# Cross-attention and feed-forward on one core: value tiles double-buffered across chunks, x converted in halves

## The reference

```
q  = (M @ Wq.T).reshape(512, 8, 64).transpose(1, 0, 2)
kv = x @ Wkv.T + bkv                       # x: 6250 x 256
k, v = jnp.split(kv, 2, axis=-1)           # each to (8, 6250, 64)
sim  = einsum('hid,hjd->hij', q, k) * 64 ** -0.5
attn = softmax(where(mask, sim, -1e9), axis=-1)
out  = einsum('hij,hjd->hid', attn, v)     # back to (512, 512)
m = layer_norm(out @ Wo.T + bo + M)
z = layer_norm(relu(m @ W1.T + b1) @ W2.T + b2 + m)
```

## Time and profile before

| | us |
|---|---|
| median of 3 runs | 763.78 (762.9 to 764.46) |
| the profiled execution | 757.08 |
| its span in the trace | 754.7 |
| PE, DVE, ACT, POOL busy in the span | 648.0, 552.9, 366.1, 243.4 |
| first reduction of a score (start of chunk 0) | 30.31 |
| start of the last chunk | 521.07 |

### The profile page before, as it was taken

How to read it: one execution, slowest core, us unless ns; L and a number is a source line. 1 busy time by engine, 2 the same in 40 slices (tenths; PEclk the granted TensorE clock), 3 DMA queues, 4 the chain that set the end, 5 groups by cost and what they waited for, 6 DMA issues and landing times.

```text
span 754.7 us, 11237 instructions
## 1 busy us (share of the span) xinstructions
PE 648.0 (86%) x3382; PEld 401.9 (53%) x3382; DVE 552.9 (73%) x688; ACT 366.1 (49%) x658; POOL 243.4 (32%) x293
## 2 busy tenths in 40 slices
PE   4867989898898989898989989898989659799995
PEld 3654545554455555455555445554545315578884
DVE  4496799778986898779987899689977732534333
ACT  4454555546555555455564555555554411333332
POOL 2221542227320532245222632054222430522223
PEclk9978999999999999999999999999999869799998
DMA  7066599857896689849986799668874981022221
GB/s 289 1 174 144 126 222 246 221 138 178 216 263 145 148 214 256 187 106 222 249 225 146 172 219 263 144 150 206 211 171 122 301 217 45 28 92 103 83 83 56
DMA packets 52504, 127.96 MB, mean 170 GB/s; under 512 B 15744, under 2 KB 16256, under 8 KB 52224
## 3 DMA queue, kind: packets, MB, share of 16 engines
q1 hardware_dynamic: 41728, 101.97, 52.6%
q10 hardware_dynamic: 10752, 25.70, 13.5%
HBM read 23.80 MB, written 1.05 MB: 33 GB/s over the span
## 4 chain that ended last, share of the span: by engine, by line
PE 49%; SPq 17%; DVE 13%; issue 8%; DMA 8%; ACT 3%; POOL 0%; DVEq 0%; ACTq 0%; POOLq 0%
SPq L335 16%; PE tail L831 12%; PE slot L804 10%; PE tail L729 9%; DVE st L658 7%; DMA pt<-st 7%; PE slot L882 6%; PE slot L890 6%; PE slot L729 5%; DVE prob L648 3%; ACT val L519 1%; DMA wq_raw<-in_wq 1%; PE slot L763 1%; PE tail L838 1%; DVE stats L682 1%
## 5 line engine op out<-in xcount | busy, mean ns | idle before, releaser
L513 ACT ACTIVATE prob<-prob,negmax 128x896 f32<-128x896 f32 x224 | 233.7, 1043 | 239.5 <-DVE negmax L648 236.4
L648 DVE CUSTOM_DVE_ANT_0 prob<-slot,lower,negmax_old 128x896 f32<-128x896 f32 x224 | 249.0, 1149 | 77.8 <-PE slot L804 68.7
L658 DVE STREAM_TRANSPOSE st<-prob 128x1792 f32<-128x1792 f32 x112 | 228.5, 2041 | 22.1 <-DMA pt<-st 20.4
L831 PE MATMUL tail<-pt,val 128*64 128x512 f32 x784 | 191.0, 622 | 20.5 <-DMA pt<-st 10.3
L804 PE MATMUL slot<-k_hi,q_hi 64*128 64x448 f32 x448 | 98.0, 429 | 34.8 <-DVE negmax L648 34.8
L831 PEld LDWEIGHTS tail<-pt,val 128*64 128x64 f32 x784 | 52.2, 142 | 125.3 <-issue 105.7
L804 PEld LDWEIGHTS slot<-k_hi,q_hi 64*128 64x128 f32 x448 | 44.6, 190 | 101.9 <-issue 93.8
L804 PE MATMUL slot<-k_hi,q_lo 64*128 64x448 f32 x448 | 87.4, 379 | 0.0
L804 PE MATMUL slot<-k_lo,q_hi 64*128 64x448 f32 x448 | 86.8, 377 | 0.0
L413 POOL TENSOR_TENSOR total<-total,alpha 128x8 f32<-128x8 f32 x28 | 5.7, 205 | 225.3 <-ACT alpha L550 225.3
L426 POOL TENSOR_TENSOR k_lo<-k_raw,k_hi 128x896 fp32r<-128x896 f32 x27 | 57.0, 2110 | 3.9 <-POOL k_hi L423 0.2
(11 more groups left out here) (110 smaller groups left out, 832.1 us busy)
## 6 DMA issues: line engine op xcount, KB each, us to landing
pt<-st SPq DMA_DIRECT2D x672, 112.0 KB, 3.0
pt<-st ACTq DMA_DIRECT2D x224, 112.0 KB, 3.4
w_raw<-in_w SPq DMA_DIRECT2D x32, 256.0 KB, 2.8
x_raw<-in_x SPq DMA_DIRECT2D x6, 896.0 KB, 5.8
mask_raw<-in_mask SPq DMA_DIRECT2D x7, 448.0 KB, 5.3
mt_raw<-in_mt SPq DMA_DIRECT2D x2, 512.0 KB, 7.8
wq_raw<-in_wq SPq DMA_DIRECT2D x2, 512.0 KB, 8.5
wo_raw<-in_wo SPq DMA_DIRECT2D x1, 1024.0 KB, 5.5
```

Source lines behind the costliest of these rows:

```text
L513: nc.scalar.activation(unit, unit, ACT.Exp, bias=negmax[:, p, u:u + 1], scale=-1.0, accum_out=psumrow[:, p, u:u + 1]).then_inc(exp_done, 1)
L648: nc.vector.tensor_tensor_reduce(out=prob[:, i % 2, h].rearrange("p (b n) -> p b n", b=2), in0=slot[:, j, :, :HALF], in1=lower[:, i].rearr ...
L658: nc.vector.transpose(st[:, g].rearrange("p b k (t i) -> p k b t i", t=2)[:, :, :, t2], prob[:, i % 2].rearrange("p h (k b i) -> p (h k) b ...
L831: last = nc.tensor.matmul(outT[DH * h:DH * h + DH], val[:, i, head(p, h)], moving, start=(i == 0), stop=(i == KT - 1))
```

## The change

The lists of rounds are new. `val` gets three more tiles (`TWICE` = 3). Value tiles 0, 1 and 2 have a second place that is used in odd chunks (`val_at`), so their copies wait only for the weighted sums of the chunk before the last one. N0 is V0 of the next chunk, done in the last round of this one, and P0 is V0 of the very first chunk. V1 to V6 then stand one to a round. All engine programs are given the chunk's parity, and the loop over chunks is unrolled by two: chunks 0, 1, a loop of two passes with two chunks each, and chunk 6.

`x_raw` has half its size. The next chunk's x comes in two DMAs of 448 KB (R0 in p0r0, R1 in p2r2). GpSimd converts the first half (J0) in p2r1 behind K and ahead of L, the second (J1) in p2r3. R1 waits until the first half has been converted. At the start of the kernel the second half lands in `x_late`, memory that is used for something else afterwards.

F and A of pairs 0 and 2 go from r1 to r2. In pair 2, W0 to W6 are spread over all four rounds. After the last chunk's values the loads of the two bias rows get a wait on `pv_done`, and two small tiles change places in memory.

```diff
+TWICE = 3
 ROUNDS = (
-    ('S E0 E1 W0 W1 W2 X M1 R',
-     'S E0 E1 Z F K H L A X B1',
-     'S E0 E1 W3 W4 W5 W6 C X M0 Q',
-     'S E0 E1 X B0'),
-    ('S E0 E1 W0 W1 W2 W3 X M1',
-     'S E0 V0 E1 Z K H L X B1',
-     'S E0 E1 F W4 W5 W6 C A X M0',
-     'S E0 V1 E1 V2 V3 X B0'),
-    ('S E0 V4 E1 W0 W1 W2 X M1',
-     'S E0 E1 Z F K H L A X B1',
-     'S E0 V5 E1 W3 W4 W5 X M0',
-     'S E0 V6 E1 W6 C X B0 J I'),
-    ('S E0 E1 W0 W1 W2 X M1',
-     'S E0 E1 Z F K H L A X B1',
-     'S E0 E1 W3 W4 W5 W6 C X M0',
-     'S E0 E1 X B0 O'),
+    ('S E0 E1 W0 W1 W2 W3 X M1 R0',
+     'S P0 E0 V1 E1 Z K H L X B1',
+     'S E0 E1 F W4 W5 W6 C A X M0 Q',
+     'S E0 E1 V2 X B0'),
+    ('S E0 E1 W0 W1 W2 W3 X M1',
+     'S E0 V3 E1 Z K H L X B1',
+     'S E0 E1 F W4 W5 W6 C A X M0',
+     'S E0 E1 V4 X B0'),
+    ('S E0 V5 E1 W0 W1 X M1',
+     'S E0 V6 E1 Z K H J0 L X B1',
+     'S E0 E1 F W2 W3 W4 A X R1 M0',
+     'S E0 E1 W5 W6 C X B0 J1 I'),
+    ('S E0 E1 W0 W1 W2 W3 X M1',
+     'S E0 E1 Z F K H L A X B1',
+     'S E0 E1 W4 W5 W6 C X M0',
+     'S E0 E1 N0 X B0 O'),
 )
...
+                elif kind in "NP":
+                    if kind == "P" and not first or kind == "N" and last:
+                        continue
+                    step = ("V", 1 if kind == "N" else 0, i)
...
-        x_raw = sb("x_raw", [P, DC, CHUNK], F32, att)
+        x_raw = sb("x_raw", [P, DC, HALF], F32, att)
-        val = sb("val", [P, KT, INNER], F32, att)
+        val = sb("val", [P, KT + TWICE, INNER], F32, att)
...
+        def val_at(kt, parity):
+            return KT + kt if kt < TWICE and parity else kt
...
                     if kind == "R":
-                        taken = in_register(sp, x_taken(c))
+                        taken = in_register(sp, x_taken(c) + i)
                         sp.wait_ge(xhi_ready, taken)
                         sp.wait_ge(xlo_ready, taken)
-                        sp.dma_start(x_raw[:], src).then_inc(x_in, 16)
+                        sp.dma_start(x_raw[:], src[:, :, i * HALF:i * HALF + HALF]).then_inc(x_in, 16)
...
+                        sp.wait_ge(klo_done, PAIRS * CHUNKS - 1)
                         sp.dma_start(wo_raw[:], wo).then_inc(wo_in, 16)
...
-                        sp.wait_ge(klo_done, PAIRS * CHUNKS - 1)
+                        sp.wait_ge(pv_done, KT * PAIRS * (CHUNKS - 1))
                         sp.dma_start(bo_sb[:], bo.to_broadcast([P, DM])).then_inc(bias_in, 16)
...
                     if kind == "J":
+                        half = slice(i * HALF, i * HALF + HALF)
-                        pool.wait_ge(v_filled, made)
-                        pool.wait_ge(filled[KEYS_RING], read)
+                        if i == 0:
+                            pool.wait_ge(v_filled, made)
+                            pool.wait_ge(filled[KEYS_RING], read)
                         pool.wait_ge(x_in, loaded)
-                        nc.gpsimd.tensor_copy(x2[0][:], x_raw[:]).then_inc(xhi_ready, 1)
+                        nc.gpsimd.tensor_copy(x2[0][:, :, half], x_raw[:]).then_inc(xhi_ready, 1)
                         pool.wait_ge(xhi_ready, taken)
-                        nc.gpsimd.tensor_tensor(x2[1][:], x_raw[:], x2[0][:], ALU.subtract).then_inc(xlo_ready, 1)
+                        nc.gpsimd.tensor_tensor(x2[1][:, :, half], x_raw[:], x2[0][:, :, half], ALU.subtract).then_inc(xlo_ready, 1)
...
                     if kind == "V":
-                        act.wait_ge(v_filled, KT * c + i + 1)
-                        if is_past(n, 1):
-                            act.wait_ge(pv_done, KT * (PAIRS * c - 1) + i + 1)
-                        nc.scalar.copy(val[:, i], tp).then_inc(v_copied, 1)
+                        own = c + p
+                        act.wait_ge(v_filled, KT * own + i + 1)
+                        if i < TWICE and is_past(own, 2):
+                            act.wait_ge(pv_done, KT * (PAIRS * (own - 1) - 1) + i + 1)
+                        if i >= TWICE and is_past(own, 1):
+                            act.wait_ge(pv_done, KT * (PAIRS * own - 1) + i + 1)
+                        nc.scalar.copy(val[:, val_at(i, parity ^ p)], tp).then_inc(v_copied, 1)
...
                         if p == PAIRS:
-                            pe.wait_ge(xhi_ready, x_taken(c + 1))
-                            pe.wait_ge(xlo_ready, x_taken(c + 1))
+                            pe.wait_ge(xlo_ready, x_taken(c) + 1)
                         for b in range(2):
+                            if p == PAIRS and b == 1:
+                                pe.wait_ge(xlo_ready, x_taken(c + 1))
                             last = keys_half(p % PAIRS, KEYS_RING, b)
...
-                            last = nc.tensor.matmul(outT[DH * h:DH * h + DH], val[:, i, head(p, h)], moving,
+                            last = nc.tensor.matmul(outT[DH * h:DH * h + DH], val[:, val_at(i, parity ^ (p < 0)), head(p, h)], moving,
```

More of the change, by code:

```diff
@@ L154, in build @@
         lower = sb("lower", [P, QT, CHUNK], BF16, att)
-        val = sb("val", [P, KT, INNER], F32, att)
+        val = sb("val", [P, KT + TWICE, INNER], F32, att)
         outT_sb = sb("outT_sb", [P, E], F32, att)
+        late = att.enter_context(ExitStack())
+        x_late = sb("x_late", [P, DC, HALF], F32, late)
+        late.close()
         prob = sb("prob", [P, 2, 2, CHUNK], F32, att)
@@ L182, in build @@
         w22 = [sb("w2_hi", [P, 2, DM], F32R), sb("w2_lo", [P, 2, DM], F32R)]
+        hid = sb("hid", [P, 2, E], F32)
+        bo_sb = sb("bo_sb", [P, DM], F32)
+        b2_sb = sb("b2_sb", [P, DM], F32)
         norm = sb("norm", [P, QT, DM], F32)
@@ L267, in chunks @@
         def chunks(eng, body):
-            body(0, chunk_schedule(True, False))
+            body(0, chunk_schedule(True, False), 0)
             mid = chunk_schedule(False, False)
-            with eng.Fori(1, CHUNKS - 1) as c:
-                body(c, mid)
-            body(CHUNKS - 1, chunk_schedule(False, True))
+            body(1, mid, 1)
+            with eng.Fori(2, CHUNKS - 2, 2) as c:
+                body(c, mid, 0)
+                body(c + 1, mid, 1)
+            body(CHUNKS - 1, chunk_schedule(False, True), 0)
         def hidden_tiles(eng, body):
@@ L396, in _, with body @@
                 lower_tile(t)
-            def body(c, sched):
+            def body(c, sched, parity):
                 final = isinstance(c, int) and c == CHUNKS - 1
@@ L427, in body @@
                     if kind == "J":
-                        read, loaded, taken = [in_register(pool, v) for v in (keys_use(pair_no(c, PAIRS - 1)) + 1, 16 * (c + 1), x_taken(c + 1))]
-                        made = in_register(pool, KT * (c + 1))
+                        half = slice(i * HALF, i * HALF + HALF)
+                        read, made = in_register(pool, keys_use(pair_no(c, PAIRS - 1)) + 1), in_register(pool, KT * (c + 1))
+                        loaded, taken = in_register(pool, 16 * (2 * c + i + 1)), in_register(pool, x_taken(c) + i + 1)
                         pool.wait_ge(zeroed, 2)
-                        pool.wait_ge(v_filled, made)
-                        pool.wait_ge(filled[KEYS_RING], read)
+                        if i == 0:
+                            pool.wait_ge(v_filled, made)
+                            pool.wait_ge(filled[KEYS_RING], read)
                         pool.wait_ge(x_in, loaded)
-                        nc.gpsimd.tensor_copy(x2[0][:], x_raw[:]).then_inc(xhi_ready, 1)
+                        nc.gpsimd.tensor_copy(x2[0][:, :, half], x_raw[:]).then_inc(xhi_ready, 1)
                         pool.wait_ge(xhi_ready, taken)
-                        nc.gpsimd.tensor_tensor(x2[1][:], x_raw[:], x2[0][:], ALU.subtract).then_inc(xlo_ready, 1)
+                        nc.gpsimd.tensor_tensor(x2[1][:, :, half], x_raw[:], x2[0][:, :, half], ALU.subtract).then_inc(xlo_ready, 1)
                     if kind == "S" and p == PAIRS - 1 and not final:
@@ L487, in _ @@
                 act.wait_ge(x0_in[b], 16)
-                nc.scalar.copy(x2[0][:, :, cols], x_raw[:, :, cols]).then_inc(xhi_ready, 1)
+                nc.scalar.copy(x2[0][:, :, cols], (x_raw, x_late)[b][:]).then_inc(xhi_ready, 1)
             for i in range(2):
@@ L779, in tp_free, with body @@
                 elif before is None:
-                    pe.wait_ge(acc_added, pair_no(c, -PAIRS) + 1)
+                    pe.wait_ge(v_copied, KT * c + 1)
                 elif before[0] == "V":
-                    pe.wait_ge(v_copied, KT * c + before[2] + 1)
+                    pe.wait_ge(v_copied, KT * (c + before[1]) + before[2] + 1)
                 else:
                     pe.wait_ge(acc_added, pair_no(c, before[1]) + 1)
-            def body(c, sched):
+            def body(c, sched, parity):
                 banks = bank_plan(sched)
```

13 lines of the change are left out of this document (5 added, 8 removed).

## The result

The changed kernel takes 711.3 us (median of 4 runs, 710.36 to 711.92); the kernel before took 763.34 beside it (4 runs, 762.62 to 764.46). The ratio is 0.932, between 0.9303 and 0.9337. The forecast was 718, its range 704 to 739.

The account below looks back on a forecast made before the run. DVE and PE each need 71.4 us of an 81.9 us chunk, the rest lost to uneven spreading of work. Gains 34.5 (middle chunks) + 5 (first) + 7 (last) = 46.5, say 46, off 763.8 give 718 us, range 704 to 739.

Parts of the forecast that it names:

- The stepping of PE against DVE: Each round lasts the longer of DVE's time and PE's pieces less its lead; middle-chunk pairs 18.3, 18.3, 19.3, 18.4, sum 74.4.
- ScalarE at the borders: Copies of V4 and outT behind both exponentials delay V5 in p2r0 and W0 in p3r0: chunk 74.4, otherwise 72.6.
- Moves: Moves pt<-st in middle chunks land nearly in time for the next pair's transpose; 0.1 us a chunk counted.
- x in halves: Two half loads of x, converted on GpSimd ahead of pair 3's key split: cost 0, at most 0.4 us.
- The missing 0.5: Stepping the old lists gave 81.4 us a chunk against 81.9 measured; the 0.5 was added to the new chunk.
- The loop unrolled by two, costed at 0: The chunk loop unrolled by two adds no time, as W and K beside it hide a few tenths.
- First and last chunk: First chunk 76 us, a gain of 5 (2 to 7); last chunk gains 7, its end after pair 2's move stays.
- The sum and the median: 46 us off: profiled execution from 757.08 to 711; median, taken as 6.7 above it, from 763.8 to 718.

Follow-up runs that it names:

- the unrolled kernel: The changed kernel with its seven chunks written out and no loop: 710.72 us, ratio 0.931.
- the second list of V tiles: The kernel before, single value buffers and x whole, with V one to a round and F kept first: 733.72 us, ratio 0.9636.
- the unrolled pair of kernels: The changed kernel with chunks written out, 710.72 us, and the same with the copies of V4 and outT also put ahead of the second exponential, 700.97 us.
- The late J0: Also called key split first: the copies first kernel with x's first half converted behind the key split in p2r1: 718.98 us, ratio 0.9432.
- The filler: The kernel before with unused repeats of V0's matmuls in p0r3 and p3r3 of every chunk, not in the last: 758.36 us, ratio 0.9949.
- copies first: The changed kernel with the copy of V4, and W5, W6 and the copy of outT, ahead of the second exponential: 703.05 us, ratio 0.9211.
- weights mid: The copies first kernel with the last chunk's weight loads behind the second move of pair 2 (p3r0): 705.89 us, ratio 0.9259.
- weights late: The late J0 kernel with the last chunk's weight loads behind the first move of pair 3 (p3r2): 727.56 us, ratio 0.9536.

## Why the prediction was right, and by how much it was not

*The stepping of PE against DVE.* Right, round by round, where moves and the jump do not disturb it. Predicted and measured in chunk 2 of the unrolled kernel: p0r1 4.78, 4.74; p2r0 4.64, 4.73; p2r1 5.45, 5.43; p3r0 4.87, 4.84; pairs 18.3, 18.4, 19.3, 18.4 and 18.30, 18.34, 19.40, 18.39. In the changed kernel itself p0r1 is 4.63 to 5.20 and p1r1 4.74 to 5.52. The bank waits of p1r3 went as forecast, and the second list of V tiles shows that cause alone.

*ScalarE at the borders.* Right: both waits are in the trace, 8.6 us before V and 5.7 before W. DVE's view of p2r1, changed kernel, chunk 2, and PE's V5 ahead of it:

```profile
218.16 0.73 PE L750 MATMUL tail<-wv_hi,x_hi 128*128 128x512 f32 x2 [1.12 <-ACT val L540]
```

```profile
223.28 1.15 DVE L669 CUSTOM_DVE_ANT_0 prob<-slot,lower,negmax_old 128x896 f32<-128x896 f32 x1 [0.55 <-PE slot L825]
```

Taking them away was expected to bring the 1.8 us a chunk between 74.4 and 72.6; the unrolled pair of kernels gives 74.54 - 73.29 = 1.25. Of the missing 0.5, 0.2 is what the prediction named as a way to be wrong: S of p3r0 waits for the key split once the copy no longer hides it (4.47 on average for 4.31). Another 0.2 is the stepping: p2r1 was put at 4.55 without the border wait and takes 4.77, the time of any other round with V and K. The rest is in p3r1, 0.14 longer than before the copies moved.

*Moves.* Right in the main: transposes waited 3.2 us for moves outside the last chunk's 11.4, in four rounds of up to 1.11, and the share is 0.86 to 0.87. That is more than the 0.1 a chunk counted. By the ceiling of 435 GB/s that the Trainium skill (DMA: Bandwidth & Descriptors, Specifications) gives, the queues would be half empty at this rate; the trace has 0.87 at 215 GB/s. The moves were in time by either, so it decided nothing here.

*x in halves.* Right that it costs nothing to be seen: SP waited 6.0 us in six times for the first half, and S waited for the key split once, 0.5 us. The late J0 shows how near the edge that is. What the halves gain was not tested in the changed kernel.

*The missing 0.5.* Mis-sized: it should have been 0. It was carried over from the kernel before without a cause. Some 0.2 of it is p0r2 behind the half-clock stretches, which are gone; the rest has no cause on record. Unrolled, a chunk is 74.54, which is 74.4 + 0.1.

*The loop unrolled by two, costed at 0.* Wrong: one round of 7.28 for 4.32, 3.0 us, 0.6 a chunk. With the loop a chunk is 75.45 against the 75.0 predicted, so 32.3 for 34.5. The four chunks without the jump average 74.98, 0.4 over the unrolled ones. The timeline puts most of that to transposes that wait for moves (p1r1 of chunk 1, first line, and two more of 0.6 to 0.7) and to the round p0r1 behind the jump, where PE is late (second line):

```profile
132.44 2.05 DVE L679 STREAM_TRANSPOSE st<-prob 128x1792 f32<-128x1792 f32 x1 [1.11 <-DMA pt<-st]
...
343.38 1.15 DVE L669 CUSTOM_DVE_ANT_0 prob<-slot,lower,negmax_old 128x896 f32<-128x896 f32 x1 [1.01 <-PE slot L825]
```

In the unrolled kernel the transposes outside the last chunk wait 0.8 us in all. Its ScalarE shows no stretch of over 1.5 us without a visible cause, the changed kernel's shows three of 2.7 to 3.4 besides the one at the jump. ScalarE issues four pieces of each move, so the loop may make the moves late too; that is not shown.

*First and last chunk.* 6.1 for 5 and 6.2 for 7; the last chunk's end stayed as said, with a transpose that waits 11.4 us for its move in both kernels.

*The sum and the median.* The profiled execution was to take 711 and took 711.92. But the forecast of the median was 718, and it is 711.3. The step that failed is the transfer: "The median of the runs shown is 763.78, 6.7 above it", taken as a constant. It is a difference between one quick execution and the others of a kernel that scatters; the changed kernel's profiled execution is 0.6 above its median. The filler shows that the empty rounds cost time; what makes the scatter is not shown. The range does not hold this: the terms named for it reach down to about 715 (first chunk 7 for 5, moves 0 for 0.1), and nothing named gives its 710. That 711.3 lies inside is luck in that respect: the gain in the traces, 44.6, was forecast as 46, and the gain in the medians was 52.0. Inside the chunk two mistakes nearly cancel: the 0.5 carried over, and the 0.9 that the loop and the late moves put on the unrolled 74.54. The "0.2%, 1.5 us, from no change" is too fine as well: the unchanged kernel against itself has an interval of 0.9929 to 1.002.

## What to carry to other kernels

Where two engines need the same time and hand over through a few slots, write down each round's work and the lead the slots allow, and step it: in the unrolled kernel it gave the rounds to a tenth, and it said that a level load, with no less work, was worth 7 us a chunk, where 6.5 came. Ask of each wait you remove which one stands right behind it, for the copies it was the key split, for the weights the bias. And when one execution is compared with a median, look first at whether the kernel scatters and with what, before a difference is carried over.

## What the chip showed that was not expected

- Adding 3.2 us of matmuls to each chunk but the last made the kernel 5.3 us faster (ratio 0.9949, 0.9912 to 0.9986), and the granted clock stayed at 1.00 over the border.
- One jump back cost 3 us when the body was two chunks; the four jumps of the loop over one chunk showed no such round. ScalarE is idle without a visible cause at that jump in all five traces with this loop, 7.57, 6.75, 6.41, 5.48 and 5.44 us (changed kernel, copies first, weights mid, key split first, weights late), and in the last two DVE's round there is 4.8 and 4.3 and the rounds behind it are the longer ones. It is idle so in neither trace with the chunks written out. Why a jump costs this is not shown. The packets on the instruction queue do not tell: 27 with this loop, 25 written out, 11 before.
- Eight loads issued ahead of a move made it land 11.10 us after its issue (chain of the changed kernel, last chunk), against 2.45. The kernel before has 10.65 there:

```profile
557.30 11.10 DMA pt<-st
```
